# The transpose of the row maxima moves to stand directly in front of a round of value products

## The reference

```
q_lat, k_lat, v_lat = q @ q2l.T + b, k @ kv2l.T + b, v @ kv2l.T + b   # latent size 32
q_lat, k_lat = rope(q_lat), rope(k_lat)
att  = einsum('bhql,bhkl->bhqk', q_lat @ wqk.T + wqk_b, k_lat) * 32 ** -0.5
att  = softmax(where(causal, att, -inf))
y    = (att @ v_lat) @ l2o.T + l2o_b          # heads side by side, then cproj
out  = x + y @ cproj.T + cproj_b + experts(layernorm(x))
```

## Time and profile before

| | |
|---|---|
| runs | 623.15 us median of 3 (617.81 to 629.47) |
| profiled execution | span 623.9 us; this one's time is its span |
| busy over the span | PE 569.5 us (91%), PEld 388.5 (62%), DVE 480.6 (77%), ACT 353.0 (57%), POOL 365.0 (58%) |
| attention, first to last transpose of maxima | 126.8 to 512.8 us, 64 of them, 6.1 us a step |

### The profile page before, as it was taken

The page is one execution under the profiler, slowest core; times in us unless marked ns, Lnnn a source line. Parts: engine busy times, 40 slices in busy tenths (PEclk is TensorE's granted clock), DMA queues, the critical chain, the costliest instruction groups (busy, mean ns, idle before and its releaser), DMA issues.

```text
span 623.9 us, 12715 instructions
## 1 busy us (share of the span) xinstructions
PE 569.5 (91%) x3562; PEld 388.5 (62%) x3562; DVE 480.6 (77%) x1679; ACT 353.0 (57%) x868; POOL 365.0 (58%) x478
## 2 busy tenths in 40 slices
PE   4979979788999999999999999999999998999991
PEld 4857747465566566556556665655655454999991
DVE  6469675676888898888889888989976777677771
ACT  4852442245777777767677676677766565223220
POOL 3300368576888676666676665766763232477774
PEclk9989999797999999999999999999999999999996
DMA  9515455968686877767777767777778864233332
GB/s 289 215 67 193 137 192 154 229 207 183 162 186 168 196 168 179 154 169 177 181 181 178 172 158 184 174 185 174 168 171 195 221 168 147 50 35 32 34 32 21
DMA packets 51371, 97.99 MB, mean 157 GB/s; under 512 B 7158, under 2 KB 26486, under 8 KB 51176
## 3 DMA queue, kind: packets, MB, share of 16 engines
q1 hardware_dynamic: 33368, 71.97, 48.8%
q10 hardware_dynamic: 11440, 20.60, 9.8%
q0 software_dynamic: 6496, 4.62, 5.7%
HBM read 26.40 MB, written 19.87 MB: 74 GB/s over the span
## 4 chain that ended last, share of the span: by engine, by line
PE 58%; DMA 11%; POOL 9%; issue 7%; ACT 6%; DVE 5%; SPq 2%; ACTq 1%; POOLq 0%; DVEq 0%
PE bank L2022 15%; PE bank L1695 13%; PE bank L1937 12%; DMA KQ<-dkq 7%; POOL out L1797 6%; PE bank L1704 4%; PE bank L1681 3%; ACT prob L1904 2%; DMA out<-ye,token 2%; PE bank L531 2%; PE bank L483 1%; PE bank L2064 1%; SPq L1600 1%; PE bank L485 1%; PE bank L1539 1%
## 5 line engine op out<-in xcount | busy, mean ns | idle before, releaser
L1733 DVE CUSTOM_DVE_ANT_0 scratch<-bank,late 128x512 bf16<-128x512 f32 (+3 forms) x512 | 234.2, 485 | 43.7 <-PE bank L1695 39.3
L1904 ACT ACTIVATE prob<-bank 128x512 f32<-128x512 f32 (+3 forms) x512 | 206.0, 437 | 83.7 <-PE bank L2022 81.1
L2022 PE MATMUL bank<-KQ 98*128 98x256 f32 (+2 forms) x512 | 182.2, 373 | 7.2 <-ACT prob L1904 6.1
L1695 PE MATMUL bank<-KQ 96*128 96x256 f32 (+2 forms) x512 | 164.4, 369 | 9.7 <-DMA KQ<-dkq 6.4
L1786 POOL TENSOR_SCALAR_AFFINE_SELECT prob<-prob 128x256 f32<-128x256 f32 x256 | 105.0, 414 | 114.9 <-ACT prob L1904 114.5
L2022 PEld LDWEIGHTS bank<-KQ 98*128 98x128 f32 x512 | 96.2, 189 | 74.3 <-ACT prob L1904 59.2
L1695 PEld LDWEIGHTS bank<-KQ 96*128 96x128 f32 x512 | 95.9, 191 | 67.8 <-issue 28.5
L1937 PE MATMUL bank<-prob,v_all 128*9 128x384 f32 (+11 forms) x1024 | 93.9, 441 | 0.7 <-POOL prob L1786 0.7
L1797 POOL DMA_INDIRECT out<-ye,token x38 | 59.5, 1565 | 32.8 <-issue 15.5
L464 POOL DMA_INDIRECT sorted_x<-xn,pos x32 | 31.6, 987 | 52.6 <-DVEq L1230 45.6
L1823 ACT ACTIVATE g<-bank 128x352 f32<-128x352 f32 x38 | 17.6, 463 | 54.8 <-PE bank L1949 54.8
(11 more groups left out here) (177 smaller groups left out, 903.1 us busy)
## 6 DMA issues: line engine op xcount, KB each, us to landing
KQ<-dkq SPq DMA_DIRECT2D x192, 256.0 KB, 3.9
stk<-latent ACTq DMA_DIRECT2D x39, 256.0 KB, 5.0
latent<-qkH SPq DMA_DIRECT2D x8, 512.0 KB, 2.8
latent<-qkL SPq DMA_DIRECT2D x8, 512.0 KB, 4.0
sorted_x<-pad_sb SPq DMA_DIRECT2D x10, 260.0 KB, 3.9
stk<-latent SPq DMA_DIRECT2D x9, 256.0 KB, 5.1
x<-in_x SPq DMA_DIRECT2D x8, 256.0 KB, 5.8
out<-x SPq DMA_DIRECT2D x8, 256.0 KB, 5.1
```

The source lines that it names most:

```text
L1695: nc.tensor.matmul(score_bank(k)[:, 0:w], KQ[0:KROWS, m % SLOTS, 1, T * b + P * q:T * b + P * (q + 1)], KQ[0:KROWS, m % SLOTS, 0, T * b:T ...
L1733: nc.vector.tensor_tensor_reduce(scratch[:, i % 2, 0:w], score_bank(k)[:, 0:w], mask[:, T - w:T], 1.0, MASKED, ALU.add, ALU.max, mx[:, m % ...
L1904: nc.scalar.activation(prob[:, n % 4, cell, at:at + PW[j]], ST[i % 2][:, lo - q0:T - q0], ACT.Exp, scale=SCALE).then_inc(exp_done, 1)
L2022: nc.tensor.matmul(ST[b][:, 0:T - q0], KQ[0:SROWS, n % SLOTS, 0, T * b + P * j:T * b + P * (j + 1)], KQ[0:SROWS, n % SLOTS, 1, T * b + q0: ...
```

## The change

Two numbers: the place of `move_maxima` in even and in odd steps. Nothing is added or taken away, and the lists of VectorE, ScalarE, GpSimd and SyncE are the same instruction for instruction.

```diff
-MAX_T_AT, PROJECT_AT, YT_AT, LATENT_AT, SUMS_AT, OUT_AT = ((4, 3), ((6, 16), (4, 16)), (8, 14), (12, 13),
+MAX_T_AT, PROJECT_AT, YT_AT, LATENT_AT, SUMS_AT, OUT_AT = ((5, 2), ((6, 16), (4, 16)), (8, 14), (12, 13),
                                                            (1, 9), (6, 5))
```

## The result

| | runs | median us | ratio to the kernel before, 95% interval |
|---|---|---|---|
| first comparison | 4 | 631.55 (628.33 to 637.12); before 625.95 | 1.013 [1.008, 1.018] |
| again | 12 | 629.03; before 625.73 | 1.009 [1.005, 1.013] |
| a third time | 12 | 630.27; before 624.91 | 1.010 [1.005, 1.015] |

So the change costs about 1%. The ratio leaves out, of each kernel, the runs over 1.5% above its own fastest, which is why it lies a little above the ratio of the medians (1.005 to 1.009). The profiled execution took 628.33 us, with a span of 626.6.

What follows compares the result with a forecast made beforehand. TensorE's list was taken to set the pace in attention. Odd-step stalls of 9.8 us less 5.0 and 1.4 given back make +3.4 on the profiled 623.9, 627.3; with the runs' median 0.75 lower, 626, range 617 to 634.

Steps and rivals of the forecast that it cites:

- the full copy: ScalarE's copy of the query latents; its end frees bank 7, for which the odd steps' transpose waits: 0.12 to 0.62 us.
- The release adds 0.04 us: Odd steps: time from the end of ScalarE's query copy to the waiting transpose, taken from an exponential's wait: 0.04 us.
- just in time: Odd steps: VectorE reads out the head's last maximum at 301.54, against the value round's old start at 301.56; no cost.
- a head like step 27: Start of odd steps 3, 7, ..., 55: 0.12 us of wait plus 0.04 after it, 0.16 us for each of 14.
- The 0.04 after the wait: Odd steps: the transpose's weight load no longer hidden after a real wait; taken as 0.04 us, bounds 0 and 0.27.
- The transpose's own 0.11 us only changes place: Odd steps: the transpose's 0.11 us of TensorE's chain moves ahead of the value round and adds nothing.
- 13 heads like step 29, with the earlier `high_k`: Odd steps 1, 5, ..., 53: nine lose 0.66 us, four 0.3; copies ending 0.40 us earlier give back in the nine.
- even steps ahead of the heads: Before nine steps like 29: ScalarE's copy end sets the time, so 0.16 us lost in the step like 27 is swallowed.
- rest of the odd steps, with the output products: Six odd steps whose output product waits 2.8 us together for VectorE's part of the maxima: half, 1.4 us, comes back.
- Rival 1: Attention: TensorE has slack and VectorE is the bound; the stall is free, up to 17.4 us go, 606.5; chance 0.12.
- Rival 2: Odd-step heads: nothing in flight after the wait, value round starts after the transpose's full 0.27 us; 18.2 us, 642; chance 0.12.
- Rival 3: Odd steps: ScalarE's list times them, so the value round moves within time TensorE waits anyway; about 623; chance 0.1.

Runs made afterwards that it cites:

- the query copies out of the way: The change plus the query latents' product two places earlier in even steps and ScalarE's two copies one exponential earlier: 659.10 us, 1.061 of the kernel before.

## Why the prediction was right and where it failed

The time lies in the range (617 to 634), the direction and the mechanism are as forecast, and the loss is within 2%. But 626 is some 4 us too low, and the loss of 1% is clear of the noise here, where the forecast had half of that.

**What was right.** That TensorE sets the pace and pays for what it stands still; that the even half gives and costs nothing (0.998 alone); that the odd half waits for the full copy, which comes last; that VectorE's gain turns into waiting for TensorE (for the projections, though, and not for S, as forecast); and that the earlier maxima give back part through the DMA waits and the output products.

**The step that failed** is the price of the wait: "The release adds 0.04 us", the start of the old value round as the point to count from, and after the wait "0.04" taken out of 0 to 0.27. With it went the last maximum, called "just in time" and so put at nothing. For a head like step 27 that made 0.16 us; it is 0.31, by two errors in the first two pieces:
- The point to count from is where the transpose would start by itself in its new place. That is 0.36 after the S (the query copies out of the way, where the last maximum is early too), not the round's 0.44. So the last maximum, at 0.42, is late by itself, and costs a head 0.26 us in steps 57 and 61, which have no copy and were put at 0.16 at most. The forecast has the transpose start at 0.56, which is 0.20 of wait and not 0.12.
- From the full copy's end to the transpose's start it is 298.41 - 298.26 = 0.15, not 0.04: the 0.04 of the earlier trace rows came from another wait. Behind the last maximum it is 0.06.

0.20 + 0.11 = 0.31. The 0.04 after the wait was nothing at all: the round follows the transpose by 0.20 with and without a wait. "The transpose's own 0.11 us only changes place" held.

**The account of the body**, sums over steps 4 to 56 against the mean of two traces before (a head from the first S to the second T, an even step from first S to first S):

| | forecast | measured (profiled execution) |
|---|---|---|
| 13 heads like step 27 | 13 x 0.16 = 2.1 | 4.2 |
| 13 heads like step 29, with the earlier `high_k` | 9 x (0.66 - 0.40) + 4 x 0.3 = 3.5 | 4.9 |
| even steps ahead of the heads | -9 x 0.16 = -1.4 | -3.0 |
| rest of the odd steps, with the output products | -1.4 | -2.5 |
| body | +2.8 | +3.6 |

The heads were 3.5 us too cheap and the give-back 2.8 too small. That these two errors nearly cancel is luck. Of the 3.0 us of the even steps 2.5 lie in those with `high_k`, whose wait for the fills is gone, and the 2.5 of the odd ones in the six with an output product, about the upper bound, 6 x 0.40. The other two traces of the change give +4.0, and the runs 4.1 at equal clock. Against the forecast's 3.4 on the profile that is not much; the rest of the 626 lay in its base, since the 623.15 that I started from was the median of three runs, and that of some hundred is 625.8. What the loss outside the body is made of, a few tenths of a microsecond, stays open; the heads of steps 57, 59 and 61 belong to it.

**Rivals.** Rival 1 (VectorE is the bound) falls: VectorE's wait for the rounded copy went to 3.0 us and the time rose. By the Trainium skill, Perfetto Trace Analysis, section Identifying the Most-Contended Engine, the weight loads' 58% meant room on TensorE (the section asks for the matmul work over the engine's peak beside it, which was not worked out). Here a stand of 0.31 us in each head was paid in full, and the measurement decides. Rival 2 gave 0.39 us for a head like step 27, and the first T is just 0.39 later; still, its reason falls. The round starts 0.20 us after the transpose, before the 0.27 us of its row are over, and does so without a wait as well; 0.08 of the 0.39 comes back by the second T; and most of the long stall in steps like 29 was given back, which its 642 leaves out. Rival 3 (nothing happens) falls by the heads.

## What to carry to other kernels

Before moving a small step forward on the engine that sets the pace, find the last of all that it waits for at the new place, and what would hold it next if that were gone, and count the stall from where the step would start there by itself, with the release as it is on that very wait. If the step must wait for something that ends a few tenths later, put it behind a batch that needs nothing (here the value round), not in front of it: the transpose behind the odd steps' round instead of in front of it (with the even steps as they were) turned a loss of 1% into a gain of 0.5 to 0.7%. What the small step itself costs depends on its neighbour, too.

## What the runs showed of the hardware

- The transpose in front of a 512-column T costs TensorE 0.11 us, 0.03 ahead of the T and 0.08 behind it; behind a value round and in front of an S, 0.01 to 0.02 (from the round to the second T 1.75 us with it in between, 1.73 in the change, 1.84 in the old order); in front of a value round 0.20 passes from its start to the round's, whose weight load begins only then (298.60 in step 27).
- A matmul that waited for ScalarE's full copy started 0.15 us after that copy's recorded end, its weight load 0.12 us after; a transpose that waited for the last maximum started 0.06 after its recorded end (step 57 of the third trace of the change); for an exponential the chain had 0.04.
- The time of a run goes with its mean granted clock: 0.55 us for each 0.001 in 24 runs of the kernel with the transpose behind the round, 0.47 in 24 of the change.
